# A transformer block on one Trainium2 core: four early loads joined and reordered, TensorE given transposes before its first data

## What is computed

```python
def rmsnorm(x, w):
    return x * jax.lax.rsqrt(jnp.mean(x * x, axis=-1, keepdims=True) + EPS) * w
def film(x, cond, w, b):
    ss = cond @ w + b
    scale, shift = jnp.split(ss, 2, axis=-1)
    return x * (1.0 + scale[:, None, :]) + shift[:, None, :]
h = film(rmsnorm(x, norm1_w), cond, film1_w, film1_b)
Q = h @ q_w + q_b; K = h @ k_w + k_b; V = h @ v_w + v_b
attn = jax.nn.softmax(jnp.einsum('bnd,bmd->bnm', Q, K) * D ** (-0.5), axis=-1)
x = x_in + (jnp.einsum('bnm,bmd->bnd', attn, V) @ proj_w + proj_b)
h = film(rmsnorm(x, norm2_w), cond, film2_w, film2_b)
out = x + gelu(h @ mlp_w1 + mlp_b1) @ mlp_w2 + mlp_b2      # x after attention
```

## Time and profile before

| | before |
|---|---|
| median of 3 runs | 234.42 us (234.26 to 234.46) |
| the profiled execution | 234.09 us, of it 232.2 us from the first to the last instruction |
| TensorE matmul busy | 218.7 us (94%) |
| VectorE busy | 148.5 us (64%) |
| ScalarE busy | 110.4 us (48%) |
| GpSimd busy | 70.9 us (31%) |
| moved by DMA | 26.72 MB |

### The profile page before, as it was taken

One profiled execution on the slowest core, in us unless ns is written; L12 is line 12 of the kernel. 1 busy time (PEld: TensorE's weight loads), 2 busy tenths in 40 slices (PEclk: granted clock), 3 DMA queues, 4 the chain that ended last, 5 costly groups with the idle time before them and its releaser, 6 DMA issues.

```text
span 232.2 us, 3530 instructions
## 1 busy us (share of the span) xinstructions
PE 218.7 (94%) x1284; PEld 190.4 (82%) x1284; DVE 148.5 (64%) x288; ACT 110.4 (48%) x207; POOL 70.9 (31%) x102
## 2 busy tenths in 40 slices
PE   0998999999889999999999899999999999999994
PEld 0767988978768999998999799888888888888994
DVE  0599767669598998989989575143724372436223
ACT  3158654425333355333363881377437743744440
POOL 1575752002325512852543224321232123200000
PEclk9999999999999999999999999999999999999999
DMA  6994000054568968654556420000200020002002
GB/s 165 342 401 181 3 12 35 3 180 139 182 220 271 259 204 265 204 181 164 182 201 236 143 57 0 3 0 0 90 3 0 0 90 3 0 0 92 3 0 90
DMA packets 15713, 26.72 MB, mean 115 GB/s; under 512 B 1872, under 2 KB 10064, under 8 KB 15568
## 3 DMA queue, kind: packets, MB, share of 16 engines
q1 hardware_dynamic: 13392, 18.11, 24.9%
q10 hardware_dynamic: 2304, 8.39, 9.4%
HBM read 16.00 MB, written 10.49 MB: 114 GB/s over the span
## 4 chain that ended last, share of the span: by engine, by line
PE 78%; DVE 9%; DMA 7%; issue 2%; SPq 2%; ACT 1%; ACTq 0%; DVEq 0%
PE psum L711 36%; PE psum L785 16%; PE psum L836 8%; PE psum L828 5%; PE psum L834 5%; DMA raw<-in_film_wT_dram 3%; PE psum L729 3%; DMA crossing<-raw 2%; PE psum L703 2%; PE psum L723 2%; DVE hT L516 1%; DMA keys_first<-crossing 1%; ACT probsT L404 1%; PE psum L833 1%; SPq L190 1%
## 5 line engine op out<-in xcount | busy, mean ns | idle before, releaser
L658 DVE TENSOR_TENSOR G_all<-probs,G_all 128x512 fp32r<-128x512 f32 x32 | 22.4, 706 | 46.3 <-ACT G_all L453 46.3
L785 PEld LDWEIGHTS psum<-V_all,probsT 128*128 128x128 f32 x384 | 47.1, 189 | 5.4 <-DVE probsT L613 4.6
L785 PE MATMUL psum<-V_all,probsT 128*128 128x256 f32 x384 | 48.3, 283 | 2.7 <-DVE probsT L613 2.6
L711 PE MATMUL psum<-hT,w 128*128 128x512 f32 x192 | 49.1, 393 | 0.0
L711 PE MATMUL psum<-hT,G_all 128*128 128x512 f32 x192 | 46.5, 393 | 0.1
L453 ACT ACTIVATE probs<-psum,vcol 128x512 f32<-128x512 f32 x32 | 22.0, 689 | 44.5 <-PE psum L711 44.4
L711 PEld LDWEIGHTS psum<-hT,G_all 128*128 128x128 f32 x192 | 35.1, 188 | 7.5 <-ACT probs L393 0.6
L711 PEld LDWEIGHTS psum<-hT,w 128*128 128x128 f32 x192 | 35.5, 188 | 6.6
L404 ACT CAST probsT<-keys_first 128x1024 fp32r<-128x1024 f32 x16 | 16.8, 1050 | 42.8 <-DMA keys_first<-crossing 16.8
L312 POOL TENSOR_TENSOR x_rows<-x_rows,add_row 128x256 f32<-128x256 f32 x16 | 11.8, 739 | 69.2 <-DVE probsT L613 69.2
L836 PE MATMUL psum<-w,G_all 128*128 128x512 f32 x84 | 30.4, 396 | 0.0
(11 more groups left out here) (70 smaller groups left out, 258.4 us busy)
## 6 DMA issues: line engine op xcount, KB each, us to landing
keys_first<-crossing SPq DMA_DIRECT2D x64, 128.0 KB, 3.0
crossing<-turned ACTq DMA_DIRECT2D x8, 512.0 KB, 4.1
crossing<-raw ACTq DMA_DIRECT2D x8, 512.0 KB, 3.5
out_dram<-x_rows SPq DMA_DIRECT2D x8, 256.0 KB, 2.0
x_rows<-in_x_dram SPq DMA_DIRECT2D x3, 512.0 KB, 9.8
raw<-in_film_wT_dram SPq DMA_DIRECT2D x2, 512.0 KB, 8.7
raw<-in_mlp_w_dram SPq DMA_DIRECT2D x1, 1024.0 KB, 7.9
raw<-in_mlp_w_dram SPq DMA_DIRECT2D x4, 256.0 KB, 4.9
```

The lines of the kernel that those rows point to most:

```text
L658: dve.tensor_tensor(gelu[:, m, LO, :], gelu_full[:, m % 2, :], gelu[:, m, HI, :].bitcast(F32), ALU.subtract).then_inc(gelu_ready, 1)
L711: last = pe.matmul(dst, stationary(a, k), moving(b, k), start=(n == len(tiles) * len(PASSES) - 1), stop=(n == 0))
L785: last = pe.matmul(bank(6 + t % 2, D), probsT[:, t % 2, a, k, :], V_all[:, t // KT * KT + k, s, :], start=(n == 0), stop=(n == KT * len(PA ...
```

## The change

x group 0 and the q·k weights are each loaded by one transfer, with one semaphore each; ScalarE's and VectorE's squares of group 0 then wait for the same semaphore. Of the conditioning rows the first is loaded alone, as third transfer, then come the film weights, then the 22 vectors; the second row is loaded alone after x group 1, and VectorE waits for it before the second film products. `wide_in` now counts only the later load of the rows, so its wait at L642 is for 16. TensorE begins with 24 transposes of the identity into two PSUM banks as soon as the identity is written, and waits for the q·k weights after them.

```diff
+    WARM = 24
...
-        wqk_in = [sem(f"wqk_in{e}") for e in range(DT)]
+        wqk_in = sem("wqk_in")
+        cond_in = [sem(f"cond_in{b}") for b in range(B)]
...
-        x_half_in = sem("x_half_in")
...
-            load(x_rows[:, 0:GT // 2, :], x_v[:, 0, 0:GT // 2, :], x_half_in)
-            load(x_rows[:, GT // 2:GT, :], x_v[:, 0, GT // 2:GT, :], x_in[0])
-            for e in range(DT):
-                load(qk_raw[:, e, :], qk_weights[:, e, :], wqk_in[e])
+            load_x(0)
+            load(qk_raw, qk_weights, wqk_in)
+            load(cond_rows[0][:, 0:1, :], rows[0:1, :].partition_broadcast(P), cond_in[0])
+            load(film_wT[0], film1_wT, film_in[0])
             load(vcol[:, :], vectors, vec_in)
-            load(cond_rows[0], rows[0:B, :].partition_broadcast(P), wide_in)
-            load(film_wT[0], film1_wT, film_in[0])
             load(raw[:, QK_END:VP_END], vp_weights, wvp_in)
             load_x(1)
+            load(cond_rows[0][:, 1:2, :], rows[1:2, :].partition_broadcast(P), cond_in[1])
             load(wk, k_w, k_in)
...
-                act.wait_ge(x_in[g] if g > 0 else x_half_in, 16)
+                act.wait_ge(x_in[g], 16)
...
-            dve.wait_ge(wide_in, 16)
+            dve.wait_ge(cond_in[0], 16)
             dve.wait_ge(film_in[0], 16)
...
+            dve.wait_ge(cond_in[1], 16)
             film_products(0, 1, late_place)
...
-                        dve.wait_ge(wide_in, 32)
+                        dve.wait_ge(wide_in, 16)
...
+            pe.wait_ge(ident_ready, 1)
+            for n in range(WARM):
+                pe.transpose(bank(n % 2)[:, 0:P], ident[:, :], ident[:, :])
+            pe.wait_ge(wqk_in, 16)
             for e in range(DT):
-                pe.wait_ge(wqk_in[e], 16)
                 for i in range(DT):
...
-            pe.wait_ge(ident_ready, 1)
             transpose_rows(0)
```

## The result

The changed kernel took 235.77 us (median of 22 executions, 234.76 to 237.12), the kernel before, run beside it, 234.59 (22 executions, 233.97 to 235.36). The ratio is 1.0056, 95% interval 1.004 to 1.0072: slower by about half a per cent. The profiled execution of after took 236.49 us (span 234.5), 2.40 more than the profiled one of before.

The account below looks back on a forecast made before the run. Bound: a film-weight DMA, then VectorE until `low_G(0)` ends at 22.1, then mostly TensorE. A 0.45 us gain at 25.32 took the profiled 234.09 to 233.64, against the median 233.97, forecast 234.0; range 233.1 to 234.9.

Parts of the forecast that it names:

- three signs of being wrong: L747 keeps 637 ns; L343 at group 2 starts after 17; x and weights land a whole microsecond earlier.
- everything behind moves by the same amount: After the handover near 22.14 us: whatever TensorE gains in its first 25 us carries through to the end.
- Up to 6.9 they are free: Head, TensorE: the 24 transposes cost nothing until the q·k weights land near 6.9 us.
- the two slower ones: Rivals: one-row broadcasts each cost as much as two rows, 235.2, chance 0.13; transposes last to 9.0, 236.2, chance 0.04.
- The clock of the weight product: Head, L747: transposes raise the clock, matmuls go from 637 to 380 ns, saving 1.8 us if ready at the higher level.
- the rival that they leave it low: Head, TensorE: the clock stays low after the transposes, 0 to 0.35 us lost, 234.5, chance 0.28.
- Larger transfers: Head loads: joining two halves into larger packets saves 0.2 us, bounds 0 to 0.94.
- One row ahead of film: Head queue: one conditioning row costs 0.64 us (0.32 to 1.27), so film lands about 1.0 us earlier.
- What is late next: Near 22 to 25 us: VectorE's 0.8 us gain is capped by x group 2's branch to 0.45 at 25.32.
- the second branch: ScalarE's wait for x group 2 until 16.80, then squares to row transposes at 25.32; landing moves only by 0.2.
- The price of two one-row broadcasts: Rival, queue ahead of x group 2: 1.27 us later at 16.80, TensorE 0.8 late at 25.32, 235.2, chance 0.13.
- 0.2 + 0.1 + 0.17: Gain at 25.32 us: larger transfers' 0.2 plus slack of 0.1 and 0.17 on x group 2's branch, given as 0.45.

Follow-up runs that it names:

- the three matmuls: Three fp32 matmuls of 512 columns (12 instructions) in place of the changed kernel's 24 transposes (48): 233.88 us, ratio 0.9988 to the kernel before.
- 16 more: Changed kernel plus 16 identity transposes behind the row transposes of group 0: 236.08 us, ratio 1.0068 to the kernel before.
- 16 inside the wait: Changed kernel plus 16 identity transposes inside TensorE's wait ahead of the third attention: 234.70 us, ratio 1.0035 to the kernel before.

## Why the prediction was wrong

Forecast 234.0 us (233.1 to 234.9), faster or the same; measured 235.77, slower. The head gained 0.24 us where 0.45 was forecast; what lies behind it was wrong. None of the three signs of being wrong that the prediction names came, since all three lie in the head.

- **The step that failed** is "everything behind moves by the same amount", with the transposes counted only as TensorE's time under the cover of the first loads ("Up to 6.9 they are free"). They are also 48 instructions that must be fetched, a term that the sum does not have. By that the 0.24 us gained at 25 us became 0.69 lost at 70.53, because the instruction packet at 64.1 made the fourth store 4.39 us long instead of 3.17; and the wait behind it took the clock as well, 1.6 us in the profiled execution. The transposes alone and the loads alone show it from both sides, the 12 transposes and the three matmuls that it is place and not work. None of the rivals had this mechanism; that the time came out slower bears out neither of the two slower ones.
- **The clock of the weight product**: right. 637 to 382 ns, end at 8.86 (8.9 forecast; that near by luck, as the weights came earlier, the transposes ended later than they did, and the span is 2.17 for 2.0). The transposes ended at 6.90, under the 7.2 allowed. With 12 of them, and TensorE idle between them and the product, the product also spans 2.01 us (median 381 ns): the transposes alone brought the higher level, so the rival that they leave it low is refuted here. The rule of the Trainium skill that spoke for it ("TensorE: Matmul & The Clock Gate", Part 4: PE-mode transpose) does not hold for these fp32 transposes.
- **Larger transfers**: mis-sized at 0.2. x group 0 was there at 5.07 for 5.55, the weights landed at 1.18 + 5.1 = 6.28 for 6.9: 0.5 to 0.6 us, in the middle of the bounds (0 to 0.94). The joined weights were also issued at 1.18, where the second half had been issued at 2.12; how much is the larger packets and how much the earlier issue was not separated.
- **One row ahead of film**: wrong in sign. Priced by bytes at 0.64; film landed at 2.12 + 7.25 = 9.37, 3.09 behind the weights, of which film is 1.32, so the row took 1.77 (its own landing, 1.65 + 6.4 = 8.05, says the same), over the upper bound of 1.27. Two rows and the vectors had taken 1.47 before. So this gave back half of what the joined loads won: film is read 0.32 earlier, not 1.0.
- **What is late next**: wrong. x group 2 no longer holds ScalarE until 16.80 but until 15.61, so the second branch did not cap the gain; VectorE's chain from film set it, and TensorE's wait stayed at 21.90 (0.38). In all ten kernels with the new loads x group 2 comes at 15.2 to 15.8, with the old loads at 16.43 and 16.80; which part of the new order brings this was not separated. The 0.24 gained came by another path than the 0.45 forecast; that the two are near is luck.
- **The price of two one-row broadcasts** (rival): the place was wrong, the price partly right. A single row is as dear as two ahead of film, but the second one, behind x group 1, moves x group 2 from 15.22 (both rows in one) to 15.69 at most, and it held nothing up. What the prediction gives for this rival, that packets and not bytes are slow, is what both rows in one transfer bear out.
- **Slips that change nothing**: 0.2 + 0.1 + 0.17 is 0.47, not 0.45, and film's load was issued three places earlier, not two.

## What to carry to other kernels

Instructions added in idle time need not be free if the kernel later runs on latency: here they shifted where TensorE's instruction blocks are fetched, and a block that fell into the start of a transfer everything waits for cost about as long as it held its DMA engine. Look at the instruction queue's packets before and after. To warm TensorE up, few long instructions move that place less than many short ones (12 left it, 48 moved it by 7 us). A wait that grows on TensorE can cost twice, once as the wait and again as the clock behind it.

## What had not been expected of the hardware

- An instruction packet of 16 KB took 0.87 to 1.35 us in the four kernels in which it fell into the start of the fourth store (1.35 in after, 1.30 with the transposes alone, 1.19 with 16 more, 0.87 with 16 inside the wait), and that 512 KB store took 4.1 to 4.4 us there instead of 3.2. At the store's end (65.5) it cost nothing.
- A broadcast of one row (128 KB) moved at 63 to 76 GB/s, one of two rows (256 KB) at 147 and 152, and both took the same time.
- The granted clock reads 1.00 in the first 11.5 us in windows in which matmuls run at the lower level (421 and 637 ns): there the instruction's duration tells the level, not that column.
- In the three kernels whose profiled execution shows TensorE idle for 2.15 to 2.46 us ahead of the third attention, the mean clock is 0.993 or less in 20 of 40 executions; in the seven kernels with 1.16 to 1.33 us there, in 2 of 79, and in none of the 80 executions of the kernel before (1.27) run beside them.
